# Recurrence and experts on one core: logits once per step, and a second unit's gate product ahead of the transpose

## The chip, the cores and the metric

The kernel runs on one core of one Trainium2 chip. The metric is the device time in microseconds of one execution. TensorE (PE, with its weight loads as PEld), VectorE (DVE), ScalarE (ACT), GpSimd (POOL) and SyncE (SP, which issues DMAs here) each run their own instructions in order and wait for each other with semaphores.

## What is computed

Four layers on x of 32 x 64 tokens of 128 values: a recurrent decoder with attention over a context of L = 64 rows, a mixture of 64 experts with a shared expert, a block of two attentions and a gated feed-forward, and a last projection. The change touches the first two.

```python
# x = x + recurrence(layernorm(x)); x = x + experts(layernorm(x)); ...
def step(carry, x):
    h, stopped = carry
    stop = jnp.logical_or(stopped, jnp.mean(x) == 0)
    logits = jnp.concatenate([x, h]) @ W_attn.T + b_attn
    aw = jax.nn.softmax(logits)
    applied = aw @ enc
    comb = jax.nn.relu(jnp.concatenate([x, applied]) @ W_comb.T + b_comb)
    h_new = jnp.tanh(comb @ W_ih.T + b_ih + h @ W_hh.T + b_hh)
    out = h_new @ W_out.T + b_out
...
topk_idx, topk_w = _route(x, router_w, e_bias)      # groups, top 4 of 8, then top 8 experts
g = jnp.einsum('th,ehi->tei', x, Wg)
u = jnp.einsum('th,ehi->tei', x, Wu)
h = jax.nn.silu(g) * u * coef[:, :, None]
moe_out = jnp.einsum('tei,eih->th', h, Wd)
```

## The kernel before

The recurrence has 64 steps, one for each token position, over 32 samples at once. The program is written as a sequence of gaps, four to a step, numbered through; `schedule()` yields them, and each engine walks the same sequence and puts its own part of each gap in its queue. The place is the gap's number in its step. 16 steps make a chunk of 512 tokens.

On PE a step is: place 0, the logits (L1803, h against `w_attnT`); place 1, the transpose of the weights `en` (L1807); place 2, 48 small products with the context (L1814, called comb products here) and the product W_hh (L1817); place 3, the product W_ih (L1820). Every fourth step place 3 also holds `x_parts` for the next four steps (L1787, L1789, L1791), which puts the x part of comb and logits and the bias into PSUM ahead of time. Between them DVE takes the negated maximum (L1300), ACT the exponential and its sum (L979), DVE the reciprocal and `en` (L1304, L1306), then `eb` (L1310, L1314) and comb (L1318), and ACT tanh (L985), which is the next h. `en` must lie twice side by side (2L = 128 columns), since one transpose serves two samples' halves. In the kernel before, the doubling starts at the weights: `w_attnT` holds W_attn twice, the logits are 128 columns wide, the exponential sums both copies, and `en` is scaled by 2.

The experts of a chunk are worked on while the recurrence runs the next chunk. 32 pairs of experts and the shared expert make 33 units a chunk, 132 in all. From gap 68 on a unit starts every second gap, so that in each step one unit stands at place 0 (called unit A here) and one at place 2 (unit B). A unit is: a gate product (six products, `wg`) and an up product (six, `wu`), both in L1874, from PE; th, a tanh of the gate, on ACT (L1018); (th + 1) x gate on DVE (L1442), then times up (L1448), which gives `gu`; times the routing coefficient on POOL (L765, called a pass here), which gives `hid`; and five gaps after its start the down product on PE (L1889, L1886 for the shared expert). DVE does its two instructions one gap after the products start, at place 1 for A and place 3 for B. Units go through buffers in pairs (`side`): a gate product waited until `gu` of the unit two before was done, and so did th.

POOL has a rule of its own. Its pass over unit A is placed at place 1 but waits for th of the next unit (`th_ready`, unit n + 2); its pass over unit B is placed at place 3 and waits for `en` of the next step. Behind the last step each pass waits for the next th.

In between stand the parts of the routing for the units to come, each half chunk over eight steps (the tables `EARLY`, `HALF`, `LAST`): projection, residual, normalisation, router, and then DVE's selection of groups and experts in many small operations (L1383 to L1433), most at places 0 and 2. At place 2 they stand behind comb and in front of unit B: L1392 to L1399 in steps 4 mod 8, L1404 to L1409 in 5, L1415 to L1423 in 6, L1429 to L1433 in 7. In steps 15 to 22 a split of loaded weights (L1474) stands there too, and in step 18 the scaling of norm weights (L1341, L1343) behind unit A.

Of the kernel before, what the change touches and what calls it, by code (L numbers as in the profile page):

```python
# [6 lines left out]
F16 = mybir.dt.float16  # L7
# [5 lines left out]
P = 128  # L13
# [37 lines left out]
def build(nc, ins, out):  # L51
# [21 lines left out]
    with ctx:  # L73
# [24 lines left out]
        b_rows = sb("b_rows", [1, 2 * L + P])  # L98
        battn_row, bout_row = b_rows[:, 0:2 * L], b_rows[:, 2 * L:]
# [270 lines left out]
        ET, HN, EXPS = slice(0, B), slice(B, 2 * B), slice(2 * B, 2 * B + 2 * L)  # L370
        LOGITS = slice(TL * B, TL * B + 2 * L)
# [192 lines left out]
        UNIT_AT = {unit_gap(m, n): (m, n) for m, n in chunk_units}  # L564
        PASS_AT = {gap + 1: u for gap, u in UNIT_AT.items()}
# [111 lines left out]
        RNN_DMAS = 15  # L677
# [254 lines left out]
        def _(act):  # L932
# [4 lines left out]
            for t in range(2):  # L937
                act.dma_start(battn_row[:, t * L:(t + 1) * L], ins["L0_xcond_b_attn"].unsqueeze(0)).then_inc(s["rnn_w_in"], 16)
# [27 lines left out]
            for i, w in enumerate((w_T, w_attnT)):  # L966
                copy(wx[:, i, 0, :], w[:, 0, :]).then_inc(s["wx_hi"], 1)
# [56 lines left out]
            for at, k, st, place in schedule():  # L1024
# [171 lines left out]
        def _(dve):  # L1196
# [74 lines left out]
            for i, w in enumerate((w_T, w_attnT)):  # L1271
                V.tensor_tensor(wx[:, i, 1, :], w[:, 0, :], wx[:, i, 0, :], sub).then_inc(s["wx_lo"], 1)
# [22 lines left out]
            def rnn(k, st, place):  # L1295
                t = k * SPC + st
                x_bank, eT, r = bank(X_BANK), bank(Y_BANK)[:, ET], rows(st)
                if place == 0:
                    dve.wait_ge(s["logits_ready"], t + 1)
                    V.tensor_reduce(nmax[r, :], x_bank[r, LOGITS.start:LOGITS.start + L], AX_X, ALU.max, negate=True)\  # L1300
                     .then_inc(s["nmax_ready"], 1)
                elif place == 1:
# [3 lines left out]
                    V.tensor_scalar(en[r, :], bank(Y_BANK)[r, EXPS], rsum[r, :], 2.0, mul, mul)\  # L1306
# [428 lines left out]
        def _(pe):  # L1735
# [43 lines left out]
            def x_parts(t):  # L1779
# [44 lines left out]
            def part(w, m, ts, p):  # L1824
                if p == "project":
# [33 lines left out]
            def unit(m, n):  # L1859
                half, q = divmod(n, DOUBLES)  # L1860
                if n in (0, DOUBLES):
                    pe.wait_ge(s["xn2T_ready"], 2 * (2 * m + half + 1))
                if first(m) and half == 0 and q % 2 == 0:
# [3 lines left out]
                for w, bk, ready in ((wg, side(m, n), "g_ps"), (wu, 2 + side(m, n), "u_ps")):  # L1867
                    if n == PAIRS:
                        for i, (u, v) in enumerate(HALVES):
                            last = mm(bank(bk), swgu[:, 0 if w is wg else 1, u, :], xn2_half(m, v), start=(i == 0), stop=(i == 2))  # L1870
                    else:
# [282 lines left out]
```

## Time and profile before

| | us |
|---|---|
| runs shown | 1011.72, 1007.26, 1012.1 (median 1011.72) |
| profiled execution | 1006.44 |
| its span | 1004.5 |
| PE busy | 902.7 (90%) |
| DVE busy | 734.0 (73%) |
| POOL busy | 564.0 (56%) |
| ACT busy | 484.8 (48%) |
| steps 0 to 17 of the recurrence | 43.7 to 173.1 |
| steps 18 to 23 | 173.1 to 218.7 |
| steps 24 to 63 | 218.7 to 505.6 |
| units behind the last step | 505.6 to 603 |
| attention, feed-forward, last projection | 603 to 1004.5 |

The profile is one execution. An engine's busy time is the time in which one of its instructions ran; the ends of matmuls are modelled, so the distance between the starts of two groups in PE's order (their pitch) is the better measure of what a group costs. The granted clock is given as a share of 2.4 GHz. A wait names the instruction whose semaphore came last.

### The profile page before, as it was taken

How to read it: one execution, taken by the hardware profiler on the slowest of the kernel's cores; microseconds unless marked ns; L12 is line 12 of the kernel's file. 1: busy time of each engine (PE TensorE's matmuls, PEld its weight loads, DVE VectorE, ACT ScalarE, POOL GpSimd, SP SyncE). 2: the span in 40 equal slices, each digit the busy share in tenths (PEclk: the TensorE clock that was granted, in tenths of full speed). 3: DMA queues.
4: the chain of work that ended last, by engine and by line, in shares of the span. 5: the costliest groups of instructions: out<-in, count | busy, mean ns of one | idle time of the engine just before them, and what ended most of it. 6: DMA issues, size and time to landing. Idle time of an engine off the chain costs nothing. (4 is left out here: it accounts for less than half of the span.)

```text
span 1004.5 us, 32078 instructions
## 1 busy us (share of the span) xinstructions
PE 902.7 (90%) x13472; PEld 715.9 (71%) x13472; DVE 734.0 (73%) x1834; ACT 484.8 (48%) x899; POOL 564.0 (56%) x516
## 2 busy tenths in 40 slices
PE   3489567999999999999999996999999999998886
PEld 3377455777877788778786785787877787877554
DVE  5666775876867667686769664878878888787665
ACT  2234323333232332323232223888888888887752
POOL 3588831334343433434354554777777876877773
PEclk9655556999999999999999997999999999999998
DMA  9212108342213232222223430000000000000001
GB/s 253 42 33 59 23 1 161 98 119 66 83 49 85 67 85 68 64 68 85 65 87 95 119 105 2 2 4 3 3 3 3 3 3 4 3 3 3 3 1 43
DMA packets 46532, 51.81 MB, mean 52 GB/s; under 512 B 22165, under 2 KB 37302, under 8 KB 46390
## 3 DMA queue, kind: packets, MB, share of 16 engines
q1 hardware_dynamic: 43472, 48.78, 18.7%
q8 instruction: 106, 1.74, 0.7%
q10 hardware_dynamic: 2918, 1.01, 0.6%
q14 instruction: 36, 0.29, 0.1%
HBM read 48.20 MB, written 1.57 MB: 50 GB/s over the span
## 5 line engine op out<-in xcount | busy, mean ns | idle before, releaser
L765 POOL TENSOR_TENSOR ex<-ex,xn 128x512 f32<-128x512 f32 x128 | 163.8, 1280 | 245.9 <-ACT thcb L1018 159.2
L1018 ACT ACTIVATE thcb<-ps 128x512 f32<-128x512 f32 x132 | 78.9, 598 | 203.5 <-PE ps L1874 197.5
L1889 PE MATMUL ps<-ex,wd 128*128 128x256 f32 x512 | 140.3, 396 | 1.3 <-POOL ex L765 0.9
L1442 DVE SCALAR_TENSOR_TENSOR ex<-thcb,ps 128x512 f32<-128x512 f32 x132 | 90.6, 686 | 48.1 <-ACT thcb L1018 43.6
L1874 PE MATMUL ps<-xnT,wg 128*128 128x256 f16 x768 | 105.8, 274 | 1.5 <-DVE ex L1448 1.4
L845 POOL TENSOR_TENSOR wd<-wd,a_sum 128x512 f32<-128x512 f32 x64 | 66.7, 1042 | 68.9 <-DVE a_sum L1573 68.7
L1874 PE MATMUL ps<-xnT,wu 128*128 128x256 f16 x768 | 105.3, 274 | 0.0
L851 POOL TENSOR_TENSOR wu<-encC,wu 128x1024 f16<-128x1024 f32 x44 | 93.7, 2144 | 12.6 <-ACT encC L1096 12.6
L1943 PE MATMUL ps<-wg,M 128*128 128x128 f16 x1536 | 97.5, 221 | 2.0 <-DVE wg L1542 2.0
L1943 PEld LDWEIGHTS ps<-wg,M 128*128 128x128 f16 x1536 | 92.4, 99 | 6.8 <-DVE wg L1542 2.4
L1814 PEld LDWEIGHTS ps<-eb,encC 128*128 128x128 f16 x3072 | 86.6, 98 | 14.1 <-DVE eb L1310 7.3
L1889 PEld LDWEIGHTS ps<-ex,wd 128*128 128x128 f32 x512 | 87.2, 190 | 12.7 <-POOL ex L765 2.3
L1978 PE MATMUL ps<-N,wg 128*128 128x512 f16 x384 | 93.7, 380 | 0.6 <-DVE ex L1555 0.5
L1448 DVE TENSOR_TENSOR ex<-ex,ps 128x512 f32<-128x512 f32 x132 | 90.7, 687 | 4.5
L1814 PE MATMUL ps<-eb,encC 128*128 128x2 f16 x3072 | 87.6, 164 | 4.9 <-DVE eb L1310 4.9
L1874 PEld LDWEIGHTS ps<-xnT,wg 128*128 128x128 f16 x768 | 73.4, 103 | 20.0 <-issue 6.5
L1874 PEld LDWEIGHTS ps<-xnT,wu 128*128 128x128 f16 x768 | 75.5, 98 | 9.0
L979 ACT ACTIVATE ps<-ps,nmax 32x128 f32<-32x128 f32 x64 | 20.8, 325 | 105.5 <-DVE nmax L1300 105.5
L1096 ACT COPY encC<-ps 128x1024 f32<-128x1024 f32 x64 | 64.8, 1012 | 5.4
L1978 PEld LDWEIGHTS ps<-N,wg 128*128 128x128 f16 x384 | 34.1, 98 | 37.4 <-DVE wg L1555 1.7
L1564 DVE TENSOR_REDUCE a_max<-ps 128x8 bf16<-128x512 f32 x64 | 43.4, 689 | 19.5 <-PE ps L1958 19.3
L1089 ACT CAST wu<-ps 128x1024 f16<-128x1024 f32 x44 | 44.5, 1012 | 20.4 <-PE ps L1978 20.4
(339 smaller groups left out, 1834.2 us busy)
## 6 DMA issues: line engine op xcount, KB each, us to landing
xn<-coef_rows SPq DMA_DIRECT2D x128, 256.0 KB, 3.9
thcb<-in_L_ffn_Wg SPq DMA_DIRECT2D x8, 256.0 KB, 3.4
thcb<-in_L_ffn_Wu SPq DMA_DIRECT2D x8, 256.0 KB, 4.0
wd<-in_L_ffn_Wd SPq DMA_DIRECT2D x2, 1024.0 KB, 10.4
xtok<-in_x SPq DMA_DIRECT2D x4, 256.0 KB, 6.0
thcb<-in_ctx SPq DMA_DIRECT2D x2, 512.0 KB, 11.0
wu<-in_L_xcond_attn_wq SPq DMA_DIRECT2D x2, 512.0 KB, 10.9
wu<-in_L_xcond_attn_wk SPq DMA_DIRECT2D x2, 512.0 KB, 10.6
```

The costliest lines, as they stand in the source:

```text
L765: nc.gpsimd.tensor_tensor(hid[:, side(m, n), :], gu[:, side(m, n), :], other, ALU.mult)\
L845: nc.gpsimd.tensor_tensor(half, half, a_sum[:, u, :].rearrange("p (m b) -> p m b", b=2).unsqueeze(3) .broadcast_to([P, 4, 2, 64]), ALU.mul ...
L851: nc.gpsimd.tensor_tensor(z[:, 1, 8 * u:8 * u + 8, :], a_Zc[:, u], z[:, 0, 8 * u:8 * u + 8, :], ALU.subtract)\
L1018: nc.scalar.activation(th[:, side(m, n), :], bank(side(m, n)), ACT.Tanh, scale=0.5 / WSCALE)\
L1096: nc.scalar.copy(a_Zc[:, u], ps[:, 2 * u:2 * u + 2, :].rearrange("p v (h d) -> p (v h) d", d=P))\
L1442: V.scalar_tensor_tensor(ga[:, :], th[:, side(m, n), :], 1.0, bank(side(m, n)), add, mul)\
L1448: V.tensor_tensor(gu[:, side(m, n), :], ga[:, :], bank(2 + side(m, n)), mul).then_inc(s["gu_ready"], 1)
L1814: last = mm(comb_ps[:, 2 * j:2 * j + 2], encC[:, u, j, :], eb[:, v, 2 * j:2 * j + 2], start=False, stop=(v == 1 and j == NPAIR - 1), skip_ ...
L1874: last = mm(bank(bk)[:, p * HT:(p + 1) * HT], w[:, 2 * q + p, u, :], xn2_quarter(m, v, half), start=(p == 0 and i == 0), stop=(i == 2), sk ...
L1889: last = mm(bank(5)[:, half * HT:(half + 1) * HT], wd[:, 2 * q + p, :], hid[:, side(m, n), p * HT:(p + 1) * HT], start=(n == 0 and p == 0) ...
L1943: m = mm(bank(b)[:, h * P:(h + 1) * P], M[a][:, u, 4 * b + h, :], a_h[:, k % 2, v, j * P:(j + 1) * P], start=(i == 0), stop=(i == 2))
L1978: m = mm(bank(2 * u + v), src[:, x, :], N[a][:, w, h:h + 4, :].rearrange("p h d -> p (h d)"), start=(i == 0), stop=(i == 2))
```

## The change

The logits are computed once: `w_attnT`, the bias row and the fp16 halves of the weights hold W_attn once, the logits and the exponential are 64 columns wide, and DVE writes `en` twice from one copy with a repeated read. The unit is taken apart into `gate_product` and `up_product`. Both gates of a step now stand at place 0: gate A, up A, gate B; up B stays at place 2. ACT takes th of unit B at place 1 instead of place 2. A gate product and a th wait only for the first DVE instruction of the unit two before (`unit_dve`, L1442), an up product for the second as before. Nothing in DVE's or POOL's order changes.

```diff
-        w_attnT = sb("w_attnT", [P, 2, 2 * L])
+        w_attnT = sb("w_attnT", [P, 2, L])
...
-        LOGITS = slice(TL * B, TL * B + 2 * L)
+        LOGITS = slice(TL * B, TL * B + L)
...
+        GATE_AT = {}
+        for m, n in chunk_units:
+            at_ = unit_gap(m, n) - unit_gap(m, n) % IDLE_GAPS
+            GATE_AT.setdefault(at_, []).append((m, n))
...
-                    act.wait_ge(s["gu_ready"], others(m, n))
+                    act.wait_ge(s["unit_dve"], others(m, n))
...
-                if at in UNIT_AT:
-                    unit(*UNIT_AT[at])
+                for m, n in GATE_AT.get(at, ()):
+                    if unit_gap(m, n) == at:
+                        unit(m, n)
+                for m, n in GATE_AT.get(at - 1, ()):
+                    if unit_gap(m, n) != at - 1:
+                        unit(m, n)
...
-                    V.tensor_scalar(en[r, :], bank(Y_BANK)[r, EXPS], rsum[r, :], 2.0, mul, mul)\
+                    V.tensor_scalar(en[r, :].rearrange("p (a l) -> p a l", a=2),
+                                    bank(Y_BANK)[r, EXPS].unsqueeze(1).broadcast_to([B, 2, L]), rsum[r, :], None, mul)\
...
-                    mm(x_bank[:, LOGITS], xs[v], wx[:, 1, u, :], start=False, stop=False, skip_group_check=True)
+                    mm(x_bank[:, LOGITS], xs[v], wxa[:, u, :], start=False, stop=False, skip_group_check=True)
...
+            def gate_product(m, n):
+                half, q = divmod(n, DOUBLES)
+                if n in (0, DOUBLES):
+                    pe.wait_ge(s["xn2T_ready"], 2 * (2 * m + half + 1))
+                if first(m) and n == 0:
+                    pe.wait_ge(s["weights_lo"], SHARED + 1)
+                if others(m, n) is not None:
+                    pe.wait_ge(s["unit_dve"], others(m, n))
+                projection(m, n, wg, 0, side(m, n)).then_inc(s["g_ps"], 1)
...
-                if at in UNIT_AT:
-                    unit(*UNIT_AT[at])
+                for u in GATE_AT.get(at, ()):
+                    gate_product(*u)
+                    if unit_gap(*u) == at:
+                        up_product(*u)
+                if at in UNIT_AT and at % IDLE_GAPS:
+                    up_product(*UNIT_AT[at])
```

PE in step 29 before, from the logits (`w_attnT`) over unit A's gate and up (`wg`, `wu`), the transpose (`ident,en`), a down product (`ex,wd`), the comb products (`eb,encC`), W_hh (`Hc,w_T`), unit B and W_ih (`comb,w_T`) to a down product:

```order
L1803 MATMUL ps<-w_attnT,Hc 32x128
L1874 MATMUL ps<-xnT,wg 128x256 x6
L1874 MATMUL ps<-xnT,wu 128x256 x6
L1807 MATMUL ps<-ident,en 128x32
L1889 MATMUL ps<-ex,wd 128x256 x2
L1814 MATMUL ps<-eb,encC 128x2 x48
L1817 MATMUL ps<-Hc,w_T 128x32
L1874 MATMUL ps<-xnT,wg 128x256 x6
L1874 MATMUL ps<-xnT,wu 128x256 x6
L1820 MATMUL ps<-comb,w_T 128x32
L1889 MATMUL ps<-ex,wd 128x256 x2
```

The same step in the changed kernel, with its own line numbers:

```order
L1811 MATMUL ps<-w_attnT,Hc 32x64
L1875 MATMUL ps<-xnT,wg 128x256 x6
L1875 MATMUL ps<-xnT,wu 128x256 x6
L1875 MATMUL ps<-xnT,wg 128x256 x6
L1815 MATMUL ps<-ident,en 128x32
L1908 MATMUL ps<-ex,wd 128x256 x2
L1822 MATMUL ps<-eb,encC 128x2 x48
L1825 MATMUL ps<-Hc,w_T 128x32
L1875 MATMUL ps<-xnT,wu 128x256 x6
L1828 MATMUL ps<-comb,w_T 128x32
L1908 MATMUL ps<-ex,wd 128x256 x2
```

Unit B's six gate products have moved from behind W_hh to ahead of the transpose, and the logits are 64 wide.

ACT before, in a step with the router's exponential (`ez`), from the xn2T copies on: th of unit A (`thcb`), the router's two operations, th of unit B, tanh (`Hc`):

```order
L1018 ACTIVATE thcb<-ps 128x512
L1003 ACTIVATE ez<-ps 128x128
L1006 ACTIVATE ez<-ez 128x128
L1018 ACTIVATE thcb<-ps 128x512
L985 ACTIVATE Hc<-ps,bh 128x32
```

And changed:

```order
L1021 ACTIVATE thcb<-ps 128x512 x2
L1006 ACTIVATE ez<-ps 128x128
L1009 ACTIVATE ez<-ez 128x128
L988 ACTIVATE Hc<-ps,bh 128x32
L982 ACTIVATE ps,esum<-ps,nmax 32x64
```

th of unit B has moved ahead of what ACT does at place 2.

## Rows read from the trace of the kernel before

**Rows 1.** Stretches: us, busy (x) of PE, PEld, DVE, ACT, POOL; PEclk, DMA, GB/s.

```profile
43.71:173.09 129.38, 99.16 (x1332) 77.83 (x1331) 84.84 (x244) 42.20 (x108) 83.22 (x73) 0.53 0.24 51
...
218.72:505.62 286.90, 283.33 (x3529) 227.35 (x3528) 206.21 (x620) 87.42 (x224) 111.65 (x103) 1.00 0.27 75
505.62:603.00 97.38, 93.53 (x699) 76.13 (x699) 71.00 (x133) 27.24 (x50) 52.73 (x46) 1.00 0.36 100
```

**Rows 2.** Waits of PE and PEld, 218.72 to 505.62: us in total, times, longest.

```profile
PE ps L1807 <- DVE en L1306: 2.0, 6, 1.2
...
PEld ps L1807 <- DVE en L1306: 12.6, 34, 1.5
```

**Rows 3.** Waits from 43.71 to 173.09; then PE's timeline around `x_parts` after step 3.

```profile
PEld ps L1807 <- DVE en L1306: 28.1, 16, 6.6
...
DVE nmax L1300 <- PE ps L1803: 12.6, 12, 2.1
...
66.54 0.51 PE L1787 MATMUL ps<-xnT,wx 128*128 128x128 f16 x3
...
67.62 1.11 PE L1768 MATMUL ps<-ident,wu 128*128 128x128 f32 x4
```

**Rows 4.** Timeline, steps 36 and 37: start, us, engine, line, what; [idle before].

```profile
310.83 0.69 DVE L1448 TENSOR_TENSOR ex<-ex,ps 128x512 f32<-128x512 f32 x1
...
311.54 0.39 PE L1817 MATMUL ps<-Hc,w_T 128*128 128x32 f32 x2
...
311.76 0.82 PE L1874 MATMUL ps<-xnT,wg 128*128 128x256 f16 x6
311.88 0.18 DVE L1392 TENSOR_TENSOR ez<-gtop 128x32 f32<-128x32 f32 x1
...
312.62 0.60 ACT L1018 ACTIVATE thcb<-ps 128x512 f32<-128x512 f32 x1 [3.45 <-PE ps L1874]
...
312.73 0.18 DVE L1399 TENSOR_TENSOR gtop<-ez 128x16 f32<-128x16 f32 x1
313.07 0.31 PE L1820 MATMUL ps<-comb,w_T 128*128 128x32 f32 x2
...
313.29 1.27 POOL L765 TENSOR_TENSOR ex<-ex,xn 128x512 f32<-128x512 f32 x1 [2.81 <-ACT thcb L1018]
...
314.25 0.41 PE L1803 MATMUL ps<-w_attnT,Hc 128*32 128x128 f32 x2
...
314.59 0.83 PE L1874 MATMUL ps<-xnT,wg 128*128 128x256 f16 x6
314.74 0.22 DVE L1300 TENSOR_REDUCE nmax<-ps 32x1 f32<-32x64 f32 x1
...
316.22 0.24 PE L1807 MATMUL ps<-ident,en 32*128 32x32 f32 x1
...
318.57 0.39 PE L1817 MATMUL ps<-Hc,w_T 128*128 128x32 f32 x2
```

**Rows 5.** By line: ns min/median/max, first and last; then timeline, 541 to 547 us.

```profile
L1392 DVE TENSOR_TENSOR ez<-gtop x8: 182/183/1071, 134.3 to 535.0; 128x32 f32<-128x32 f32 x8
...
L1429 DVE TENSOR_SCALAR csum<-csum x8: 157/160/867, 157.6 to 553.4; 128x2 f32<-128x2 f32 x8
...
L1318 DVE TENSOR_SCALAR comb<-ps,bcomb x64: 243/251/252, 47.9 to 510.1; 128x32 f32<-128x32 f32 x64
...
541.28 1.27 POOL L765 TENSOR_TENSOR ex<-ex,xn 128x512 f32<-128x512 f32 x1 [1.84 <-DVE ex L1448]
...
546.11 1.27 POOL L765 TENSOR_TENSOR ex<-ex,xn 128x512 f32<-128x512 f32 x1 [2.05 <-DVE ex L1448]
546.21 1.31 DVE L1412 SCALAR_TENSOR_TENSOR masked<-grank,sfc 128x128 f32<-128x128 f32 x1
```

**Rows 6.** DVE's timeline in step 18.

```profile
177.69 1.62 DVE L1341 TENSOR_SCALAR ss<-ss,norm_b 128x32 f32<-128x32 f32 x6
...
179.58 0.25 DVE L1318 TENSOR_SCALAR comb<-ps,bcomb 128x32 f32<-128x32 f32 x1
```

More of the change, by code:

```diff
@@ L936, in _ @@
                 act.dma_start(sbuf[:, :], ins[name]).then_inc(s["rnn_w_in"], 16)
[L937 to L938 removed]
+            act.dma_start(battn_row, ins["L0_xcond_b_attn"].unsqueeze(0)).then_inc(s["rnn_w_in"], 16)
             act.dma_start(bout_row, ins["L0_xcond_b_out"].unsqueeze(0)).then_inc(s["rnn_w_in"], 16)
@@ L965, in _ @@
             evacuated(act, 1)
-            for i, w in enumerate((w_T, w_attnT)):
-                copy(wx[:, i, 0, :], w[:, 0, :]).then_inc(s["wx_hi"], 1)
+            for half, w in ((wx, w_T), (wxa, w_attnT)):
+                copy(half[:, 0, :], w[:, 0, :]).then_inc(s["wx_hi"], 1)
             act.wait_ge(s["rnn_w_in"], 16 * RNN_DMAS)
@@ L1270, in _ @@
             dve.wait_ge(s["wx_hi"], 4)
-            for i, w in enumerate((w_T, w_attnT)):
-                V.tensor_tensor(wx[:, i, 1, :], w[:, 0, :], wx[:, i, 0, :], sub).then_inc(s["wx_lo"], 1)
+            for half, w in ((wx, w_T), (wxa, w_attnT)):
+                V.tensor_tensor(half[:, 1, :], w[:, 0, :], half[:, 0, :], sub).then_inc(s["wx_lo"], 1)
             V.tensor_tensor(rows16[:, 1, :], b_rows[:, :], rows16[:, 0, :], sub).then_inc(s["wx_lo"], 1)
@@ L1857, in part, with projection @@
                     last.then_inc(s["coefT_ps"], 1)
-            def unit(m, n):
+            def projection(m, n, w, shared, bk):
+                half, q = divmod(n, DOUBLES)
+                if n == PAIRS:
+                    for i, (u, v) in enumerate(HALVES):
+                        last = mm(bank(bk), swgu[:, shared, u, :], xn2_half(m, v), start=(i == 0), stop=(i == 2))
+                    return last
+                for p in range(2):
+                    for i, (u, v) in enumerate(HALVES):
+                        last = mm(bank(bk)[:, p * HT:(p + 1) * HT], w[:, 2 * q + p, u, :], xn2_quarter(m, v, half),
+                                  start=(p == 0 and i == 0), stop=(i == 2), skip_group_check=True)
+                return last
+            def gate_product(m, n):
                 half, q = divmod(n, DOUBLES)
@@ L1866, in unit @@
                     pe.wait_ge(s["gu_ready"], others(m, n))
[L1867 to L1871, printed above, removed]
-                        for p in range(2):
-                            for i, (u, v) in enumerate(HALVES):
-                                last = mm(bank(bk)[:, p * HT:(p + 1) * HT], w[:, 2 * q + p, u, :], xn2_quarter(m, v, half),
-                                          start=(p == 0 and i == 0), stop=(i == 2), skip_group_check=True)
-                    last.then_inc(s[ready], 1)
+                projection(m, n, wu, 1, 2 + side(m, n)).then_inc(s["u_ps"], 1)
             def down(m, n):
```

26 lines of the change are left out of this document (14 added, 12 removed).

## The prediction, made before the changed kernel ran

> **What bounds the kernel now.** I read first the stages, then what TensorE waits for in them, then one step of the recurrence on all engines, then how GpSimd and VectorE (DVE) disturb each other. [rows 1] cuts the span: steps 0 to 17 (43.7 to 173.1 us, clock 0.53), steps 24 to 63 (218.7 to 505.6, clock 1.00) and the expert units behind the last step (505.6 to 603); steps 18 to 23 lie between, attention behind. In steps 24 to 63 PE is busy 283.3 of 286.9 us, so a step is as long as the work in PE's order plus one wait that recurs: for `en`, in front of the transpose [rows 2]. In steps 0 to 17 the clock is at its lower level (1.2 of 2.4 GHz), PE is busy 99 of 129 us, and the chain logits, maximum, exponential, `en`, transpose, comb, tanh sets the end: DVE sat idle until the logits came 12 times, PE's loads until `en` came 16 times [rows 3].
>
> [rows 4] shows step 36 from its W_hh product on, and step 37 up to its own. W_hh starts at 311.54, gate B 311.76, W_ih 313.07, the logits 314.25, gate A 314.59, the transpose 316.22, the next W_hh 318.57: 7.03 us. Gate and up of one unit take 313.07 - 311.76 = 1.31, 0.65 each. From the logits to the transpose there are 1.97, of which 0.34 + 1.31 are work; of the other 0.32 some 0.09 is there too in steps in which `en` is early (the switch to a 32-row transpose), so the wait is 0.2. GpSimd's pass over unit A starts at 313.29, and not at 311.52 when DVE has finished unit A: it waits for th of unit B (ACT, 312.62 + 0.60) and so runs beside the two instructions of DVE that read PSUM.
>
> **The change, part by part.** (1) *Logits of 64 columns.* Their pitch is 0.34 for 2 x 128 columns; W_hh with 2 x 32 has 0.22 [rows 4]. So 96 columns cost 0.12 and 64 cost 0.08; by proportion of all columns it would be 0.17. I take 0.10 at full clock, twice that (0.21) at the low one. The exponential reads 64 columns less: ACT needs 0.60 for 512 [rows 4], so between 0 and 0.075; I take 0.03, since most of a small operation is fixed. `en` writes 128 columns as before: nothing. x_parts, once in four steps, is 1.08 us long at the low clock [rows 3] and loses half the columns of five of its eight products: between 0 and 5/16 of it, 0.34; I take 0.2 there and 0.1 at full clock. One 1-row DMA and some setup columns less lie under the load and the normalisation of x, and shorten only DVE's last operations before step 0: 0.2 once.
> Early stage: 12 steps released by the logits [rows 3] x (0.21 + 0.03) = 2.9, x_parts 3 x 0.2 = 0.6, one more step bound by PE 0.2, setup 0.2: **-3.9 us**. In the other steps DVE is late by itself and nothing is gained.
>
> (2) *Gate B in front of the transpose.* 0.65 us of PE work moves from behind W_hh to ahead of the transpose. The new cover from logits to transpose is 0.24 + 3 x 0.65 + 0.09 = 2.29 (with rounding), against a chain of 0.39 to the maximum and 1.48 on (314.74 to 316.22): the wait is gone where DVE is on time. Between W_hh and W_ih there is then 0.22 + up B 0.65 = 0.87 instead of 1.53. comb is ready some 0.45 behind W_hh (the routing operations behind it start at 0.34), so of 1.1 us of slack 0.4 is left and no new wait arises. A step without a wait is 2.29 + 2.35 (transpose to W_hh) + 0.87 + 1.18 (W_ih to logits) = 6.69.
>
> (3) *What the move releases.* th of B now follows a product ahead of the transpose: gate B starts 1.55 behind the logits, ACT 0.86 later, 0.60 long, ready at 3.0. That was the late wait of GpSimd's pass A, which now goes when DVE has finished unit A, beside W_hh, and lasts 1.27. DVE's queue holds next: comb, the routing operations of place 2, unit B, and the next step's maximum. The routing operations read two SBUF tensors, or are TENSOR_SCALARs in SBUF, and the trace shows what a pass of GpSimd does to such: L1412 1.31 us, to the end of GpSimd's pass that began 0.1 before it; L1392 1.07 instead of 0.18; L1429 0.87 instead of 0.16 [rows 5]. comb, which reads PSUM, never took over 0.25, though GpSimd was busy 83 of 129 us in the first stage [rows 1, 5].
> Price at step 36: GpSimd from 311.6 to 312.87 holds L1392 (begun 311.88) to 312.9; the six others need 0.93 as before (311.98 to 312.91), to 313.8; unit B 2 x 0.72, to 315.27. The next logits start at 311.54 + 0.87 + 1.18 = 313.59; their maximum could start at 313.94 and does at 315.3; the transpose comes 1.48 later, 316.78, where PE's own work ends at 315.88: a wait of 0.9. From logits to logits: 3.19 + 2.35 + 0.87 + 1.18 = 7.59 instead of 7.03, **+0.55**. Place 2 carries about 1 us of such operations in the steps with number mod 8 = 4, 5, 6 and 7. The steps behind 4, 5 and 6 lose 0.55 each; behind 7 the output projection stands in PE's order ahead of the transpose and covers it. The other five steps of eight gain: 0.10 each, the waits of two of them (0.2), x_parts (0.2): 0.9. A cycle is 1.65 - 0.9 = +0.75. Five cycles: +3.7. Step 51 holds the longest wait, 1.2 [rows 2], and sheds 0.5 of it. **+3.2.**
> One of the held operations, L1415, is a TENSOR_SCALAR over 128 columns that never ran beside GpSimd here: between not held (5 x 0.5 = 2.5 us less) and held. The nearest row is L1429, also a TENSOR_SCALAR, held, so I take held. The Trainium skill (SBUF — State Buffer, Who interferes with whom) says a tensor_scalar in SBUF can take a second port pair that GpSimd shares, and that whichever of the two starts first blocks the other for its whole length. By that rule it is held and the sum stays; exempt, the sum would be 2.5 us lower.
>
> (4) *Steps 18 to 23.* In step 18, 1.8 us of TENSOR_SCALARs (L1341 and one more) stand between unit A and comb [rows 6]. GpSimd would now start with them: between nothing and a whole pass, 1.27, and straight into comb, which was already late; held like L1429: +1.2, less 0.1. Steps 19 and 20 gain 0.7. Steps 21 to 23 have the held operations and a weight split of 0.68 behind them: +0.8 each. **+2.8.**
>
> (5) *Behind step 63* PE's order changes in the same way with no chain to cover. GpSimd's passes already start right behind DVE there (541.28) and already hold a routing operation per unit or so [rows 5]. Between -1 and +6 (the rival below); I take **0**.
>
> Sum: -3.9 + 3.2 + 2.8 - 0 = **+2 us**. The profiled execution took 1006.44 (span 1004.5): 1008.4. The three runs shown (1007.26 to 1012.1, median 1011.72) lie up to 5.7 above it; with their median it would be 1013.7. I take 1011, between the two. Some 0.5% (5 us) is what a measurement of this kernel can tell from no change.
>
> **The rivals.** *Not held (0.24, faster).* GpSimd's pass misses the routing operations: it starts behind them, or they begin first. Then unit B of step 36 ends at 314.4, the maximum is 0.5 late, and 2.29 covers it. A cycle is 1.8 us shorter than now: 5 x 1.8 + 0.5 = 9.5, steps 18 to 23 some 3, early 3.9: 990 by the profiled time, 995 by the median. For it: the waits of [rows 2] are real, and the diff moves nothing in DVE's or GpSimd's order. Against: pass A is kept back by nothing but th [rows 4], and [rows 5].
> *The end of the routing (0.18, slower).* Behind step 63 DVE is near its limit in the routing. If pass A too comes to lie on a routing operation in each pair of units, up to six more are held for 1 us each: +6, 1014 by the profile, 1017 to 1020 by the median. It decides if pass A there waits for th of B today; the row at 541.28 waits for DVE, which speaks against.
> *The width of the logits saves nothing (0.08, slower).* If loading weights sets the pitch, 0.10 in 29 steps and 0.21 in 13 are missing: +5.7, 1014 by the profile. Against: W_hh has larger weights and 0.22.
> *The forecast*: 0.50.
>
> **How the numbers follow.** Faster 0.24 (the first rival), same 0.50 (the forecast), slower 0.26 (the two others). The range goes from the upper part of the first rival, 993, to the second by the median, 1020; about 2 in 10 lie outside.
>
> **What would show it.** Right: the logits' pitch 0.24; no wait for `en` in the steps 1 to 4 mod 8; pass A within 0.1 us of the end of unit A in every step; L1392 and its like at 0.9 to 1.1 us where they stand first behind comb; a wait of 0.8 to 1.0 before the transpose in the steps 5 to 7 mod 8; 290 us for steps 24 to 63 and 125.5 for steps 0 to 17. Wrong: those operations at 0.2 to 0.3 us (first rival); a stage behind step 63 of over 100 us (second); a pitch of 0.34 (third).

## The result, and the profile after

The changed kernel takes **1026.45 us** (median of 4 runs, 1024.5 to 1028.02), the kernel before 1010.68 beside it; the ratio is 1.0147, 95% interval 1.0113 to 1.0181. It is slower by 1.5%, where 1011 was forecast and 1020 was the upper end of the range. Of the ten runs of `e10_free_one` below, one took 4577.62 us and is left out of its median; no other run of this document stands out like that.

The changed kernel cut at the starts of the logits of steps 0, 18, 24 and 63, as in [rows 1] (us, busy (x) of PE, PEld, DVE, ACT, POOL; PEclk, DMA, GB/s):

```profile
43.30:170.70 127.40, 95.00 (x1332) 78.31 (x1331) 86.58 (x245) 41.34 (x108) 85.13 (x73) 0.52 0.24 51
170.70:223.34 52.64, 47.02 (x546) 37.13 (x547) 42.43 (x113) 15.64 (x40) 16.74 (x14) 0.91 0.39 98
223.34:521.70 298.36, 284.51 (x3529) 231.76 (x3528) 222.96 (x620) 83.29 (x224) 112.11 (x103) 0.98 0.26 70
521.70:620.10 98.40, 95.20 (x698) 77.59 (x698) 70.12 (x134) 27.15 (x50) 52.61 (x45) 0.97 0.36 98
```

Against [rows 1], the profiled executions differ like this:

| part | before | after | change | predicted |
|---|---|---|---|---|
| up to step 0 | 43.71 | 43.30 | -0.4 | -0.2 |
| steps 0 to 17 | 129.38 | 127.40 | -2.0 | -3.7 |
| steps 18 to 23 | 45.63 | 52.64 | +7.0 | +2.8 |
| steps 24 to the start of 63 | 286.90 | 298.36 | +11.5 | +3.2 |
| experts behind it | 97.38 | 98.40 | +1.0 | 0 |
| attention, to the end | 401.50 | 405.90 | +4.4 | 0 |
| span | 1004.5 | 1026.0 | +21.5 | +2 |

The profiled execution of before (1006.44) lies 4.2 under its median, that of after (1027.86) 1.4 above: of the 21.4 between the two, 15.8 are the distance of the medians. Most runs of the kernel before have a granted clock of 0.910 to 0.919 over the whole span and take 1010 to 1016 us, where the profiled one has 0.924. No such run was profiled, so [rows 1] does not show where the clock is lower in them.

Two things stand out at once. DVE is busy 222.96 us in steps 24 to 63 instead of 206.21, though it has no instruction more (620 both times); and the clock, 1.00 there and in steps 18 to 23 before, is 0.98 and 0.91. The waits in the same stretch, which answer to [rows 2] (us in total, times, longest):

```profile
PE ps L1815 <- DVE en L1313: 12.5, 15, 0.9
PE ps L1864 <- DVE left L1441: 1.4, 2, 0.7
...
PEld ps L1815 <- DVE en L1313: 18.0, 20, 1.2
```

PE itself waits for `en` 12.5 us instead of 2.0, in three steps of every eight and in step 51. And it waits for something that it did not wait for before: the transposes of the routing coefficients (L1864) wait for DVE's `left` in two steps, 47 and 55.

The changed kernel's steps 36 and 37, as in [rows 4]: unit A ends on DVE at 320.5, PE's W_hh is at 320.52.

```profile
319.82 0.69 DVE L1456 TENSOR_TENSOR ex<-ex,ps 128x512 f32<-128x512 f32 x1
...
320.52 0.39 PE L1825 MATMUL ps<-Hc,w_T 128*128 128x32 f32 x2
...
320.64 1.27 POOL L769 TENSOR_TENSOR ex<-ex,xn 128x512 f32<-128x512 f32 x1 [1.82 <-DVE ex L1456]
320.70 0.25 DVE L1326 TENSOR_SCALAR comb<-ps,bcomb 128x32 f32<-128x32 f32 x1 [0.19 <-PE ps L1822]
...
320.87 1.09 DVE L1400 TENSOR_TENSOR ez<-gtop 128x32 f32<-128x32 f32 x1
...
321.40 0.31 PE L1828 MATMUL ps<-comb,w_T 128*128 128x32 f32 x2
...
322.58 0.30 PE L1811 MATMUL ps<-w_attnT,Hc 128*32 128x64 f32 x2
...
323.56 0.69 DVE L1456 TENSOR_TENSOR ex<-ex,ps 128x512 f32<-128x512 f32 x1
...
324.28 0.22 DVE L1307 TENSOR_REDUCE nmax<-ps 32x1 f32<-32x64 f32 x1
...
325.70 0.24 PE L1815 MATMUL ps<-ident,en 32*128 32x32 f32 x1 [0.75 <-DVE en L1313]
```

GpSimd's pass over unit A now waits for DVE's unit A (`<-DVE ex L1456`) and no longer for th of unit B; it starts 0.12 behind W_hh. comb, which reads PSUM, takes its usual 0.25. The first routing operation behind it, L1400, takes 1.09 instead of the 0.18 of [rows 4], and ends (321.96) where the pass ends (321.91). Everything behind it on DVE is 0.9 late: the logits stand ready at 322.58 + 0.30, the maximum starts at 324.28, and the transpose comes 3.12 behind the logits, with 0.75 of wait. That is the mechanism of part (3) of the prediction, with its size.

It happens to whatever routing operation comes first in that place, not only to L1400 (the medians of L1412 and L1423, the first ones of steps 5 and 6 mod 8, are 1.18 and 1.12). By line, as in [rows 5] and [rows 6] (ns min/median/max):

```profile
L1400 DVE TENSOR_TENSOR ez<-gtop x8: 186/1085/1091, 129.7 to 554.0; 128x32 f32<-128x32 f32 x8
...
L1437 DVE TENSOR_SCALAR csum<-csum x8: 157/1060/1062, 155.7 to 571.5; 128x2 f32<-128x2 f32 x8
...
L1349 DVE TENSOR_SCALAR ss<-ss,norm_b x6: 233/241/1250, 175.5 to 177.9; 128x32 f32<-128x32 f32 x6
...
L1811 PE MATMUL ps<-w_attnT,Hc x128: 219/243/316, 43.3 to 521.8; 128*32 128x64 f32 x128
```

The medians of L1392 and L1429 in [rows 5] were 183 and 160 ns. L1349 is the TENSOR_SCALAR of step 18 ([rows 6], L1341): one of its six is held for 1.25. The logits' row gives single products by their modelled ends; from the logits to gate A in the timeline there are 0.23 (398.90 to 399.13 in step 47), where 0.24 was predicted and 0.34 was the pitch before.

**What the prediction did not have.** First, in step 47 the held operation is L1437, and three operations behind it stands `left`, which the coefficient transposes need:

```profile
404.87 1.06 DVE L1437 TENSOR_SCALAR csum<-csum 128x2 f32<-128x2 f32 x1
...
406.37 0.38 DVE L1441 TENSOR_TENSOR left<-coef,csum 128x128 f32<-128x128 f32 x1
...
406.81 0.41 PE L1864 MATMUL ps<-ident,left 128*64 128x128 f32 x2 [0.68 <-DVE left L1441]
...
407.05 1.03 PE L1908 MATMUL ps<-ex,wd 128*128 128x256 f32 x4
...
408.01 0.30 PE L1811 MATMUL ps<-w_attnT,Hc 128*32 128x64 f32 x2
```

In PE's order they stand ahead of a down product and the next logits. So the logits come 2.60 behind W_ih, 0.74 later than in the kernels below in which nothing holds L1437 (1.86). Step 55 is the same.

Second, TensorE's clock. Steps 31, 39, 47 and 55 are the same place of four cycles; then two stretches around step 23 (columns as in the first fence), and two groups of step 31:

```profile
276.60:286.51 9.91, 9.00 (x98) 7.22 (x97) 8.09 (x23) 2.21 (x6) 2.53 (x2) 0.83 0.19 61
337.81:347.73 9.92, 9.01 (x98) 7.28 (x97) 8.09 (x23) 2.21 (x6) 2.53 (x2) 0.83 0.34 95
398.90:408.01 9.11, 7.52 (x98) 6.12 (x97) 8.09 (x23) 2.21 (x6) 2.53 (x2) 1.00 0.31 82
459.76:468.88 9.12, 7.53 (x99) 6.13 (x98) 8.10 (x23) 2.21 (x6) 2.53 (x2) 1.00 0.24 65
...
217.00:222.00 5.00, 5.00 (x71) 4.35 (x70) 4.31 (x9) 0.55 (x2) 1.45 (x2) 0.57 0.62 161
222.00:226.00 4.00, 4.00 (x16) 2.43 (x15) 0.70 (x3) 0.50 (x3) 0.92 (x1) 0.50 0.69 165
```

```profile
282.45 1.43 PE L1875 MATMUL ps<-xnT,wu 128*128 128x256 f16 x6
...
284.77 0.63 PE L1864 MATMUL ps<-ident,left 128*64 128x128 f32 x2
```

The steps at a granted clock of 0.83, with part of them at the lower level of 1.2 GHz, are 0.8 longer than those at 1.00. In step 31 the lower level begins at up B (1.43 instead of the usual 0.82), and everything from there to the next logits is slow; the transposes come so late that `left` (there since 284.45) is no longer waited for. So in steps 31 and 39 the lower clock stands in the place of the transposes' wait, and 0.8 is what it costs beyond it. Around step 23 the clock stays low for some 10 us: step 24 takes 9.67 where step 32 takes 7.57. Before each fall lie steps in which PE waited for `en`; in [rows 1] the clock is 1.00 from step 24 on. In step 23 PE waited 1.38 for `en`; from 218 to 228 us the clock is low.

### The profile page after: what moved, and what is told of

Read it like the earlier page. It is cut to its first block and busy times, and to the rows that moved or that the text cites. A ratio compares the mean times of both kernels' runs of the same rounds, so it can differ in the third digit from the quotient of the medians.

```text
span 1026.0 us, 32073 instructions
## 1 busy us (share of the span) xinstructions
PE 909.6 (89%) x13470; PEld 728.6 (71%) x13470; DVE 756.2 (74%) x1834; ACT 478.7 (47%) x899; POOL 564.3 (55%) x516
## 5 line engine op out<-in xcount | busy, mean ns | idle before, releaser
L1908 PE MATMUL ps<-ex,wd 128*128 128x256 f32 x512 | 143.4, 403 | 0.6 <-DVE xT L1465 0.6
L1021 ACT ACTIVATE thcb<-ps 128x512 f32<-128x512 f32 x132 | 76.4, 597 | 84.5 <-PE ps L1875 74.8
L1875 PE MATMUL ps<-xnT,wu 128*128 128x256 f16 x768 | 109.6, 281 | 0.0
L1875 PE MATMUL ps<-xnT,wg 128*128 128x256 f16 x768 | 108.2, 278 | 1.3 <-DVE ex L1450 1.3
L1908 PEld LDWEIGHTS ps<-ex,wd 128*128 128x128 f32 x512 | 89.8, 195 | 11.7 <-DVE xT L1465 0.9
L1456 DVE TENSOR_TENSOR ex<-ex,ps 128x512 f32<-128x512 f32 x132 | 90.7, 687 | 9.2 <-PE ps L1875 3.7
L988 ACT ACTIVATE Hc<-ps,bh 128x32 f32<-128x32 f32 x64 | 18.4, 287 | 163.7 <-PE ps L1828 163.7
L1875 PEld LDWEIGHTS ps<-xnT,wu 128*128 128x128 f16 x768 | 78.0, 106 | 12.0 <-issue 0.6
L982 ACT ACTIVATE ps<-ps,nmax 32x64 f32<-32x64 f32 x64 | 17.4, 272 | 129.7 <-DVE nmax L1307 129.7
L1103 ACT COPY encC<-ps 128x1024 f32<-128x1024 f32 x64 | 64.8, 1012 | 5.4
## 6 DMA issues: line engine op xcount, KB each, us to landing
thcb<-in_ctx SPq DMA_DIRECT2D x2, 512.0 KB, 11.3
```

The source lines that it names most:

```text
L1021: nc.scalar.activation(th[:, side(m, n), :], bank(side(m, n)), ACT.Tanh, scale=0.5 / WSCALE)\
L1103: nc.scalar.copy(a_Zc[:, u], ps[:, 2 * u:2 * u + 2, :].rearrange("p v (h d) -> p (v h) d", d=P))\
L1456: V.tensor_tensor(gu[:, side(m, n), :], ga[:, :], bank(2 + side(m, n)), mul).then_inc(s["gu_ready"], 1)
L1875: last = mm(bank(bk)[:, p * HT:(p + 1) * HT], w[:, 2 * q + p, u, :], xn2_quarter(m, v, half), start=(p == 0 and i == 0), stop=(i == 2), sk ...
L1908: last = mm(bank(5)[:, half * HT:(half + 1) * HT], wd[:, 2 * q + p, :], hid[:, side(m, n), p * HT:(p + 1) * HT], start=(n == 0 and p == 0) ...
```

## The experiments

The theory: GpSimd's pass over unit A, set free by the early th, is the one cause of the loss, by three ways: (a) the waits for `en` in steps 5 to 7 mod 8 and 21 to 23, (b) the wait of the coefficient transposes, (c) the lower clock that comes with them. The rivals: the new order on PE or the width of the logits costs by itself; (b) is the larger part; the pass matters only together with the earlier gate.

Lengths of one cycle of eight steps (number mod 8 = 0 to 7), logits to logits, where the clock was 1.00 throughout: steps 40 to 47, but steps 32 to 39 of `e2_logits_only`, and in `e3_before_free_pass` steps 40 to 44 and 53 to 55 (its steps 45 to 47 have a fall of the clock). Each number is the distance of two starts of the logits in the timeline.

| kernel | 0 | 1 | 2 | 3 | 4 | 5 | 6 | 7 | sum |
|---|---|---|---|---|---|---|---|---|---|
| before | 7.68 | 7.07 | 7.56 | 7.63 | 6.88 | 7.03 | 7.05 | 7.83 | 58.73 |
| after | 7.57 | 6.97 | 7.45 | 7.24 | 6.71 | 7.53 | 7.70 | 9.11 | 60.28 |
| e6_hold_tanh | 7.56 | 6.98 | 7.44 | 7.24 | 6.72 | 6.71 | 6.79 | 7.46 | 56.90 |
| e2_logits_only | 7.57 | 6.95 | 7.45 | 7.48 | 6.72 | 6.99 | 7.04 | 7.69 | 57.89 |
| e3_before_free_pass | 7.67 | 7.08 | 7.55 | 7.63 | 6.89 | 7.52 | 7.65 | 8.44 | 60.43 |
| e8_gate_move_only | 7.67 | 7.08 | 7.56 | 7.48 | 6.82 | 6.82 | 6.82 | 7.62 | 57.87 |
| e10_free_one | 7.56 | 6.98 | 7.44 | 7.25 | 6.71 | 6.71 | 7.69 | 7.46 | 57.80 |

**e1_hold_dve.** The changed kernel with pass A held until DVE has done its first instruction of unit B; nothing else.

```diff
-                        pool.wait_ge(s["th_ready"], m * UNITS + n + 2)
+                        pool.wait_ge(s["unit_dve"], m * UNITS + n + 2)
```

> The changed kernel with one wait on GpSimd exchanged: during the recurrence the pass over unit A waits until DVE has done the first instruction of unit B, not for th of unit B. Theory A (the pass falls on the routing operations behind comb and so delays en): the operations that follow comb (L1400, L1412, L1423, L1437) are back at 0.2 to 0.3 us, the wait before the transpose in steps 5 to 7 mod 8 goes from 0.8-1.0 to under 0.4 (the pass now lies on the small operations at place 0, which may hold en by 0.3), TensorE's clock stays at its upper level from step 18 to 63, and steps 24 to 63 take 277 to 282 us instead of 298; in all 1000 to 1006 us. Theory B (splitting gate and up, or the earlier th, costs by itself, for instance in bank order or on ACT): nothing moves by over 3 us, 1022 to 1028.

Measured: 999.02 us, ratio to before 0.9864 (0.9832 to 0.9895). Steps 24 to 63 in 278.54 at a clock of 1.00, steps 18 to 23 in 45.20. One line on GpSimd turns 1.5% of loss into 1.4% of gain. PE's order is that of the changed kernel, so the order costs nothing by itself.

**e6_hold_tanh.** The same, but held until h's tanh of the step.

```diff
-                        pool.wait_ge(s["th_ready"], m * UNITS + n + 2)
+                        pool.wait_ge(s["h_ready"], t + 2)
```

> The changed kernel, the pass over unit A released by tanh of the same step, which comes about 1.5 us behind W_hh: behind most routing operations of place 2 and ahead of those of place 0. Theory A: both groups of operations free, no wait before the transpose over 0.2 except in step 51, steps 24 to 63 at 276 to 279 us, steps 18 to 23 at 42 to 44, in all 993 to 1000 us and at least as fast as the release by DVE. Theory B: 1022 to 1028.

Measured: **994.32 us**, ratio 0.9827 (0.9791 to 0.9864). Its stages from step 18 on, then the place of [rows 4] in its timeline:

```profile
170.70:215.64 44.94, 42.69 (x547) 35.03 (x547) 37.52 (x113) 15.66 (x40) 18.53 (x14) 1.00 0.36 97
215.64:493.43 277.79, 277.15 (x3528) 227.15 (x3528) 203.76 (x619) 84.85 (x224) 111.31 (x104) 1.00 0.28 77
```

```profile
306.90 0.18 DVE L1400 TENSOR_TENSOR ez<-gtop 128x32 f32<-128x32 f32 x1
...
308.15 1.27 POOL L769 TENSOR_TENSOR ex<-ex,xn 128x512 f32<-128x512 f32 x1 [3.29 <-ACT Hc L988]
...
308.69 0.69 DVE L1456 TENSOR_TENSOR ex<-ex,ps 128x512 f32<-128x512 f32 x1
```

L1400 is back at 0.18, the pass lies beside DVE's instruction that reads PSUM, and PE is busy 277.15 of 277.79 us. A cycle is 1.83 shorter than before; the rival "not held" had said 1.8. Between this kernel and the changed one, which differ by that wait alone, lie 20.6 us in steps 24 to 63: 3.38 per cycle without the clock, 15.2 in all, and 5.3 of lower clock beyond that (0.8 in each of steps 31 and 39, 1.65 in step 62, 2.1 in step 24).

**e2_logits_only.** The changed kernel with gate and up of unit B together again behind W_hh, and th in its old place; the narrow logits stay.

```diff
-                for m, n in GATE_AT.get(at, ()):
-                    if unit_gap(m, n) == at:
-                        unit(m, n)
-                for m, n in GATE_AT.get(at - 1, ()):
-                    if unit_gap(m, n) != at - 1:
-                        unit(m, n)
+                if at in UNIT_AT:
+                    unit(*UNIT_AT[at])
...
-                for u in GATE_AT.get(at, ()):
-                    gate_product(*u)
-                    if unit_gap(*u) == at:
-                        up_product(*u)
-                if at in UNIT_AT and at % IDLE_GAPS:
+                if at in UNIT_AT:
+                    gate_product(*UNIT_AT[at])
                     up_product(*UNIT_AT[at])
```

> The changed kernel with gate and up of a unit together again and th at its old place: of the change only the 64-column logits are left (and the looser wait of gate and th). Both theories: per step 0.10 less at the upper clock and 0.2 to 0.3 at the lower; steps 0 to 17 about 2 us less than before, steps 24 to 63 about 5 less (282), in all 1002 to 1005 us where before is 1010.7; GpSimd's pass stays behind th, at W_hh + 1.75, and no routing operation at place 2 is held. If the width gave nothing, it is at 1009 to 1012.

Measured: 1006.99 us, ratio 0.9941 (0.9917 to 0.9965), 2 over the expectation. The profiled execution is one of the two shortest of eight (1000.51, with a granted clock of 0.922 over the span; the six others have 0.909 to 0.915), so it can't say where the 2 lie. In it the clock was low in step 21, which took 8.89 instead of 7.28, and steps 24 to 63 took 282.93: -3.97, and 0.84 per cycle, 0.10 a step as predicted.

**e3_before_free_pass.** The kernel before; the wait of pass A for th is taken out, since the pass does not read it.

```diff
-                        pool.wait_ge(s["th_ready"], m * UNITS + n + 2)
+                        pass
```

> The kernel before, with nothing changed but that GpSimd's pass over unit A no longer waits for th of unit B in the recurrence, so that it starts when unit A is done, beside W_hh. Theory A: the first routing operation behind comb is held to 0.9-1.1 us, unit B ends 0.5 to 0.9 later where they stand (4 to 7 mod 8), steps 5 to 7 mod 8 become 0.3 to 0.5 longer, step 18 about 1.2, the coefficients' transposes of step 7 mod 8 wait for DVE: in all 8 to 15 us slower than before, 1019 to 1026. Theory B: the same as before, 1008 to 1012.

Measured: 1026.01 us, ratio 1.0137 (1.0103 to 1.0172). The old kernel with one wait less is as slow as the changed one. First the held operation, then steps 46 and 54, the same place in two cycles:

```profile
L1392 DVE TENSOR_TENSOR ez<-gtop x8: 185/1033/1082, 131.4 to 552.7; 128x32 f32<-128x32 f32 x8
```

```profile
390.56:399.81 9.25, 8.50 (x88) 6.60 (x87) 7.68 (x22) 2.01 (x5) 2.54 (x2) 0.82 0.36 99
453.08:460.73 7.65, 6.89 (x89) 5.55 (x88) 6.61 (x21) 2.01 (x5) 2.54 (x2) 1.00 0.25 70
```

Held as in the changed kernel, and the clock falls here too, in steps 30, 38, 46 and 62 but not in 54. A cycle costs +1.70 without a fall and 2.7 (61.43, steps 40 to 47) with one. Steps 5 and 6 of the cycle are 7.52 and 7.65 long here, 7.53 and 7.70 in the changed kernel, though PE has the gate in different places: once an operation is held, DVE's chain sets the step, and the moved gate brings nothing.

**e4_coefT_late.** The changed kernel with the coefficient transposes behind the down product on PE.

```diff
-                for what in PRO.get(at, ()):
-                    part(*what)
+                late = [what for what in PRO.get(at, ()) if what[3] == "coefT"]
+                for what in PRO.get(at, ()):
+                    if what not in late:
+                        part(*what)
                 if at in DOWN_AT:
                     down(*DOWN_AT[at])
+                for what in late:
+                    part(*what)
```

> The changed kernel with one part moved on TensorE: in the gap of the coefficients' transposes (place 3 of step 7 mod 8) the down product goes first and the transposes behind it. Theory A (besides the held operations, these transposes wait in TensorE's own order for DVE's last routing operation, and the down product and the next logits stand behind them): step 7 mod 8 goes from 9.1 to 8.2-8.5 us, one or more of the falls of TensorE's clock behind it are gone, steps 24 to 63 lose 4 to 9 us of their 298; in all 1012 to 1021 us. Rival (the transposes' wait is free, and the falls of the clock come from elsewhere): 1024 to 1028.

Measured: 1026.93 us, ratio 1.0146 (1.0109 to 1.0184): no gain, the theory's 1012 to 1021 was wrong. Its step 55:

```profile
472.36 1.13 PE L1908 MATMUL ps<-ex,wd 128*128 128x256 f32 x4
473.33 0.38 PE L1864 MATMUL ps<-ident,left 128*64 128x128 f32 x2
473.64 0.30 PE L1811 MATMUL ps<-w_attnT,Hc 128*32 128x64 f32 x2
...
474.26 0.37 PE L1838 MATMUL ps<-rows,ones 1*128 1x256 f16 x2 [0.32 <-ACT coefT L1014]
```

The wait is gone, though L1437 is still held there (1.06), and the logits come 1.93 behind W_ih instead of 2.61. But step 56 takes 7.94 instead of 7.56: the output projection (L1838) now waits for ACT's copy of the transposes. So 0.3 a cycle is left, 1.5 in all. Steps 24 to 63 took 300.37, 2.0 more than in the changed kernel: the clock was low in steps 31, 39, 40, 47 and 54 (10.0 in step 47 instead of 9.11, 10.86 and 10.01 in steps 39 and 40). Before them it was low in steps 17 to 19 and 22. Whether moving the transposes has a part in these falls was not tested. The transposes' wait is real, and moving them did not pay.

**e7_hold_tanh_coefT.** e6_hold_tanh with the same move of the transposes.

> The pass over unit A released by tanh, and the coefficients' transposes behind the down product. With the pass held, the last routing operation is in time, so the transposes wait for little: 992 to 996 us, within 2 us of the kernel with the release by tanh alone.

Measured: 998.97 us, ratio 0.9876 (0.9844 to 0.9909), 4.7 over e6_hold_tanh and 2.4 over the same kernel in e12_hold_tanh_again, more than expected. Steps 24 to 63 take 279.95, +2.2: steps 0 and 7 of the cycle are 7.94 and 7.54 instead of 7.56 and 7.46. Steps 18 to 23 take 48.11 at a clock of 0.93 instead of 44.94 at 1.00 (46.55 at 0.96 in e12_hold_tanh_again).

**e8_gate_move_only.** The kernel before, with the gate moved and the pass held for h's tanh, and the logits 128 wide. These are parts of the diff against the changed kernel; the other lines give the weights, the bias, `en` and `x_parts` back their old width.

```diff
-        ET, HN, EXPS = slice(0, B), slice(B, 2 * B), slice(2 * B, 2 * B + L)
-        LOGITS = slice(TL * B, TL * B + L)
+        ET, HN, EXPS = slice(0, B), slice(B, 2 * B), slice(2 * B, 2 * B + 2 * L)
+        LOGITS = slice(TL * B, TL * B + 2 * L)
...
-                        pool.wait_ge(s["th_ready"], m * UNITS + n + 2)
+                        pool.wait_ge(s["h_ready"], t + 2)
```

> Logits of 128 columns as before; the gate of unit B in front of the transpose, and the pass over unit A released by tanh. Measures the move alone with its collision taken away. If the two parts of the change add: 994.3 + (1011.9 - 1007.0) = 999, some 12 less than before. If the move only paid together with the narrow logits: 1004 to 1008.

Measured: 1004.57 us, ratio 0.9939 (0.9914 to 0.9964), which speaks for the parts not adding up. The stages say otherwise: a cycle is 0.86 shorter than before here, 0.84 in e2_logits_only and 1.83 in e6_hold_tanh; steps 24 to 63 are 4.5, 4.0 and 9.1 shorter. They add up there, to 0.1 a cycle. What does not is steps 18 to 23: 48.15 at a clock of 0.93, 46.26 at 0.96, 44.94 at 1.00.

**e9_half_pass.** The changed kernel, with pass A over half its columns in the recurrence: the other half of those units' products is left out.

```diff
+                c = slice(0, CT // 2) if short else slice(0, CT)
-                nc.gpsimd.tensor_tensor(hid[:, side(m, n), :], gu[:, side(m, n), :], other, ALU.mult)\
+                nc.gpsimd.tensor_tensor(hid[:, side(m, n), c], gu[:, side(m, n), c], other[:, c], ALU.mult)\
...
-                    unit(m, n)
+                    unit(m, n, place == 1 and t < T)
```

> The changed kernel with GpSimd's pass over unit A cut to half of its columns in the recurrence (256 of 512; the output is then wrong in those columns), about 0.65 us instead of 1.27, started at the same moment. Theory A: the first routing operation behind comb is held only to the end of the short pass, 0.4 to 0.5 us instead of 1.06, the wait before the transpose in steps 5 to 7 mod 8 shrinks by 0.6 to about 0.2-0.3, and the whole lies between the changed kernel and the one with the pass held back: 998 to 1006 us. Rival (the earlier start of the pass matters, not its length): 1020 to 1028.

Measured: 1003.56 us, ratio 0.993 (0.9903 to 0.9958). The held operation and the passes, by line:

```profile
L1401 DVE TENSOR_TENSOR ez<-gtop x8: 188/546/745, 129.6 to 535.1; 128x32 f32<-128x32 f32 x8
...
L770 POOL TENSOR_TENSOR ex<-ex,xn x128: 724/1267/1312, 170.3 to 600.5; 128x512 f32<-128x512 f32 x82, 128x256 f32<-128x256 f32 x46
```

The pass goes from 1.27 to 0.72, and the operation held by it (L1400 with one line more) from 1.09 to 0.55: it lasts to the end of the pass. The step behind it (37, 45 and 53) goes from 7.53 to 6.98.

**e10_free_one.** e6_hold_tanh, but the pass free in one step of eight.

```diff
-                        pool.wait_ge(s["h_ready"], t + 2)
+                        if t % 8 == 5 and t > 23:
+                            pool.wait_ge(s["th_ready"], m * UNITS + n + 2)
+                        else:
+                            pool.wait_ge(s["h_ready"], t + 2)
```

> GpSimd's pass A is held until h's tanh, as in the best kernel so far (994.32, steps 24 to 63 in 277.8), in all steps but those with number mod 8 = 5 from step 29 on, where it goes free (on th) as in the changed kernel. One wait for en per cycle of eight steps, of 0.82. Theory (each wait costs its own length, and TensorE's clock falls only where waits follow in several steps): 4 free steps up to 63 and one more (61): 5 x 0.82 = +4.1, steps 24 to 63 in 281.9, no lower clock between steps 24 and 63, about 998.5. Rival (any single such wait brings the clock down in its cycle): 0.8 to 2.1 more per cycle, steps 24 to 63 in 285 to 290 and 1003 to 1008.

Measured: 1000.65 us (median of nine runs, 997.78 to 1006.86), ratio 0.9913 (0.9885 to 0.9941). Steps 24 to 63:

```profile
215.37:497.69 282.32, 277.15 (x3529) 227.19 (x3528) 208.25 (x619) 84.48 (x224) 111.27 (x104) 1.00 0.28 76
```

Only the step behind the free pass changes, 6.79 to 7.70; 5 x 0.91 = 4.5 us, all of 282.32 - 277.79, and the clock stays at 1.00. The median is 2 us over the expectation; its profiled execution has 1000.25 and 1.8 more than e6_hold_tanh behind step 63.

**e11_free_early.** The pass free up to step 23, held from 24 on (`if t < 24` in the same place).

> Pass A goes free up to step 23 and is held for h's tanh from step 24 on. Theory: steps 18 to 23 as in the changed kernel (52.6 instead of 44.9, a lower clock behind them, step 24 about 2.1 longer), steps 25 to 63 as in the best kernel: +7.7 + 2.1 = +9.8, about 1004. Of those, 3 to 4 us are the lower clock and vanish if the lower clock doesn't follow here: then 1000. Rival (what happens up to step 23 changes the cycles behind it too, by the phase of the queues): over 1008.

Measured: 1005.95 us, ratio 0.9939 (0.9912 to 0.9965).

```profile
171.47:224.07 52.60, 47.69 (x546) 37.49 (x546) 42.45 (x113) 15.90 (x40) 16.75 (x14) 0.90 0.34 85
224.07:501.83 277.76, 277.14 (x3528) 227.16 (x3527) 203.69 (x619) 85.01 (x224) 111.16 (x103) 1.00 0.29 77
```

The median is 2 over the expected 1004 and under the 1008 of the rival. Steps 18 to 23 cost the 52.6 of the changed kernel, with the low clock in other steps (18, 19 and 22 instead of 19, 23 and 24), and nothing of it reaches the cycles behind.

**e12_hold_tanh_again.** The kernel of e6_hold_tanh once more.

> The best kernel once more, to see if its gain stands: 993 to 997, 0.983 of before; steps 24 to 63 in 277.8, no lower clock between steps 18 and 63.

Measured: 996.53 us, ratio 0.9862 (0.9834 to 0.9889). The gain stands: in both measurements this kernel is faster than the kernel before (ratios 0.9827 and 0.9862). Steps 24 to 63 take 277.76, and steps 18 to 23 46.55. But the first of these two rows is its step 18, the second that of e6_hold_tanh, the same code:

```profile
171.66:181.56 9.90, 9.32 (x93) 7.16 (x93) 6.80 (x21) 3.74 (x10) 3.63 (x4) 0.83 0.31 82
```

```profile
170.70:178.99 8.29, 7.71 (x93) 6.28 (x94) 6.79 (x21) 3.63 (x10) 3.65 (x4) 1.00 0.41 104
```

The expectation of no lower clock behind step 18 was wrong: the lower clock of the first stage reaches into step 18 in one execution and not in the other, 1.6 us.

## Why the prediction was wrong

- **(1) Logits of 64 columns.** Right at full clock: the pitch is 0.23, and 0.10 a step at full clock is what e2_logits_only measured (0.84 in eight steps). In the early stage, steps 0 to 2 went from 5.99, 5.94 and 5.95 to 5.60, 5.67 and 5.68, 0.3 instead of 0.24 each. The stage gained 2.4 with what lies ahead of it, not 3.9: step 13 took 11.75 instead of 8.82, with DVE's L1333 and L1337 at 1.61 and 1.04 instead of 1.22 and 0.17 beside GpSimd's 512-column operations (L748, L750); step 10, where less was held than before, took 10.54 instead of 12.57. The prediction took the collisions of this stage as fixed; its term of -3.9 was mis-sized by 1.5.
- **(2) The gate in front of the transpose.** Right where DVE is on time: 6.71 for step 4 of the cycle, where 6.69 was said, and -0.86 a cycle in e8_gate_move_only. The 0.09 in front of the transpose is 0.13 in step 36 of the changed kernel (2.31 from the logits, of which 0.23 and 3 x 0.65 are work), where `en` had been ready for 0.7; that a switch of rows is its cause is shown by no run.
- **(3) The held routing operations.** The mechanism, its place and its size were right: the pass 0.12 behind W_hh, L1400 1.09, L1437 1.06, the waits in steps 5, 6 and 7 and steps of 7.53 and 7.70 where 7.59 was said. Step 51 shed the 0.5 (7.84 instead of 8.73, in a place where the others shed 0.39). The step that failed is the sum of the cycle, +0.75; it was +1.55 without the lower clock. "Behind 7 the output projection stands in PE's order ahead of the transpose and covers it" looked at the transpose and not at what else in PE's order waits for DVE's late end in step 7: the coefficient transposes, 0.74 a cycle at full clock (steps 47 and 55). The operations they wait for are the very ones that were counted as held.
- **The clock.** No term and no rival had it. It was told of the first stage only, as a level, and taken for 1.00 from step 18 on. In steps 24 to 63: 4 x 1.55, 0.3 for the last seven steps and -0.5 for step 51 are 6.0; the lower clock is 5.3; together 11.3 of the 11.5 measured. So of the 8.3 that were missing there some 3 are the transposes and 5 the clock, if a full-clock cycle is taken off first. As waits the transposes show in two of the four cycles only (1.5 us); in steps 31 and 39 the lower clock stands in their place, and the 0.74 there can be put down to either.
- **(4) Steps 18 to 23.** Step 18 +1.2 (said +1.1), 21 and 22 +0.85 and +0.91 (said +0.8). Steps 19 and 20 were to gain 0.7 and lost 0.9: the clock is low at 182 to 185, in step 19. Step 23 lost 3.1 instead of 0.8: 1.6 up to W_hh, with a wait for `en` of 1.38 instead of 0.50, and 1.5 from there to the next logits, at the lower clock and though up B is alone there; the coefficient transposes waited for nothing in it. The term was +2.8 and measured +7.0.
- **(5) Behind step 63.** +1.0 in the experts, near the 0 taken; the second rival did not happen. The stage begins with step 63, in which L1437 is held too (1.06) and the transposes wait 1.09: they come 6.93 behind the logits instead of 5.98, which is as much as the stage lost. Attention, +4.4 at a clock of 0.96 instead of 0.98, has the same code in both; e6_hold_tanh and e3_before_free_pass have 498.9 and 499.3 from step 63 to the end like before (498.9), where the changed kernel has 504.3; the nine others have 496.5 to 501.3. Whether that is more than one execution's scatter stays open.
- **The rivals.** "Not held" gave 990 to 995: no operation was unheld here, but it is what the kernel does when the pass is kept away (994.32). The chance of slower, 0.26, was put on two mechanisms that did not occur. The one that did was the forecast's own, priced with one of three consequences.

Shown by runs: that the free pass is the whole loss (e1, e6, e3), that the parts of the change are each worth some 4 us in steps 24 to 63 without it (e2, e8), that the held time is that of the pass (e9). The hold alone on the kernel before was not run. Argued from the traces only: the split between waits and clock, since no run has the one without the other at will, and that the waits bring the clock down. Kernels without these waits have a lower clock at times too: e7, e8 and e12 in steps 18 to 23, and six of the eight runs of e2 over the span (0.909 to 0.915 instead of 0.922), at places that are not known.

## What to carry to other kernels

When a change makes an input ready earlier, look for who was kept in place by its lateness: here a wait that the GpSimd pass did not need for its data ordered it behind DVE's SBUF operations, and an edit on PE took that order away. Put such an order in the code by a wait that says so (here on h's tanh), beside instructions of DVE that read PSUM. And when an operation on DVE gets later by a microsecond, price every instruction of TensorE that waits for something behind it in DVE's queue, not the nearest alone; then ask whether the waits, repeated over steps, still leave TensorE its full clock.

## What the hardware showed that was not expected

TensorE's granted clock fell inside a stretch in which PE was busy over 95% of the time. In steps 24 to 63 it never fell in the profile of before and in the seven in which PE waited for `en` for at most 0.3 in steps 5 to 7 of the cycle (e1, e2, e6, e7, e8, e11, e12), nor in e10 with one wait of 0.9 a cycle, though it did in some of them in steps 18 to 23. It fell where waits of 0.6 to 0.9 stood in two or three steps in a row: in e3 in the second of them, four times in five cycles, in e4 in steps 31, 39, 40, 47 and 54, in the changed kernel in steps 31, 39 and 62; and once, in step 30, with waits of 0.2 and 0.4 (e9). It did not fall in steps 47 and 55 of the changed kernel, whose rows read the same. A fall made its step 0.8 to 1.65 us longer, the long one around step 23 made step 24 alone 2.1 longer. What decides between a cycle with a fall and one without stays open.

A DVE operation with two operands in SBUF, or a TENSOR_SCALAR there, that began 0.2 behind a pass of GpSimd ended with the pass or up to 0.15 later: 1.27 of pass made 0.18 into 1.09, 0.72 made it 0.55. The Trainium skill (SBUF — State Buffer, Who interferes with whom) has this as an exclusive port pair that whoever begins first keeps for its whole instruction; the traces agree, for 128x2 elements (L1437, 1.06) as for 128x32.
